# A unit's last attention step issued after one score group instead of two, and edge-pass loads cut in halves

## What is computed

```python
x = layernorm(x + attn(x, wq, wk_down, wv_down, wk_up, wv_up, wo))     # causal, T = 2048
nodes = {-1: x}
for c in range(6):
    nsrc = min(c + 1, 5); snode = c - nsrc
    q = ew[c,0] * (nodes[c-1]            @ We[eq] + be[eq])
    k = ew[c,1] * (nodes[snode]          @ We[ek] + be[ek])
    v = ew[c,2] * (nodes[snode + nsrc//2] @ We[ev] + be[ev])
    nodes[c] = act_w[c] * mha(q, k, v, Wq[c], Wk[c], Wv[c], Wo[c]) + q   # 8 heads of 128
x = layernorm(x + layernorm(nodes[5], ln_g, ln_b))
```

## Time and profile before

| what | value |
|---|---|
| median of 2 unprofiled runs | 8644.6 us (8638.22 to 8650.98) |
| the profiled execution's own time | 8620.5 us |
| its span on the slowest core (core 5) | 8619.4 us |
| spans of the eight cores | 8589.2 to 8619.4 us |
| mean granted TensorE clock, all cores | 0.809 to 0.813 of full speed |
| busy: PE, ACT, DVE, POOL | 70%, 28%, 20%, 1% |
| instructions | 67350 |
| DMA, mean over the span | 32 GB/s |

### The profile page before, as it was taken

How to read it: one execution, slowest core, us unless ns; L and a number is a source line. 1 busy time by engine, 2 the same in 40 slices (tenths; PEclk the granted TensorE clock), 3 DMA queues, 4 the chain that set the end, 5 groups by cost and what they waited for, 6 DMA issues and landing times.

```text
span 8619.4 us, 67350 instructions; the slowest of 8 cores (8589.2 to 8619.4 us)
## 1 busy us (share of the span) xinstructions
PE 6007.5 (70%) x22250; PEld 2193.1 (25%) x22250; DVE 1745.8 (20%) x2473; ACT 2453.4 (28%) x2040; POOL 59.1 (1%) x71
## 2 busy tenths in 40 slices
PE   6455577767776777877768967779777788646554
PEld 3111132222332222322223412224222233212111
DVE  3332122111121111131112131111301112231133
ACT  0222212433113332123441124331133421223322
POOL 0000000000000000000000000000000000000000
PEclk8677687888887888978889978889788889768777
DMA  3000031000320002310003200012200023000000
GB/s 74 25 25 25 10 83 25 10 10 10 74 49 5 20 10 43 90 25 10 10 10 74 69 15 10 10 44 69 49 15 10 10 44 91 13 25 0 25 25 20
DMA packets 148339, 271.72 MB, mean 32 GB/s; under 512 B 5216, under 2 KB 54688, under 8 KB 148022
## 3 DMA queue, kind: packets, MB, share of 16 engines
q0 software_dynamic: 69680, 111.42, 7.9%
q10 hardware_dynamic: 64928, 113.25, 4.1%
q1 hardware_dynamic: 13414, 42.76, 1.5%
HBM read 286.55 MB, written 67.11 MB: 41 GB/s over the span
## 4 chain that ended last, share of the span: by engine, by line
PE 58%; ACT 19%; DVE 10%; issue 7%; DMA 4%; DVEq 1%; ACTq 0%; SPq 0%; POOLq 0%
PE psS L57 27%; PE psA L57 22%; ACT Dm L57 15%; PE psY L57 5%; PE psM L57 4%; ACT rowb L57 3%; DVE LNw L57 3%; DVE Dm L57 2%; DVE rowb L57 2%; DVE psS L57 1%; DMA x1w<-x 1%; DMA A<-nsc 1%; DVE mask_sb L57 1%; DVE x1w L57 1%; DMA B<-x1b 1%
## 5 line engine op out<-in xcount | busy, mean ns | idle before, releaser
L57 ACT ACTIVATE Dm<-psS,negC 128x2048 bf16<-128x2048 f32 x848 | 1668.3, 1967 | 2844.5 <-PE psS L57 2645.6
L57 PE MATMUL psS<-A,B 128*128 128x512 bf16 x3392 | 1061.8, 443 | 707.0 <-ACT Dm L57 682.7
L57 PE MATMUL psY<-Dm,Cv 128*128 128x512 bf16 x1696 | 586.8, 482 | 360.2 <-DVE Dm L57 314.2
L57 DVE CAST mask_sb<-rowb 1x512 bf16<-1x512 f32 x192 | 79.7, 415 | 3718.1 <-ACT rowb L57 3718.1
L57 PE MATMUL psA<-Dm,Cv 128*128 128x512 bf16 x1696 | 570.8, 471 | 370.9 <-DVE Dm L57 328.0
L57 PE MATMUL psA<-Dm,Wb 128*128 128x512 bf16 (+1 forms) x2624 | 645.1, 403 | 83.6 <-DVE Dm L57 78.7
L57 PEld LDWEIGHTS psS<-A,B 128*128 128x128 bf16 x3392 | 337.0, 105 | 1411.2 <-issue 1299.5
L57 PE MATMUL psM<-Dm,on_b 128*1 128x512 bf16 x1808 | 573.0, 439 | 162.2 <-ACT Dm L57 154.4
L57 PE MATMUL psS<-Dm,Wb 128*128 128x512 bf16 (+1 forms) x2624 | 593.1, 379 | 0.0
L57 PE MATMUL psA<-Dm,on_b 128*1 128x512 bf16 (+1 forms) x1712 | 563.9, 461 | 8.0 <-DVE Dm L57 8.0
L57 PE MATMUL psA<-A,Wb 128*128 128x512 bf16 x1280 | 308.6, 397 | 157.2 <-DMA A<-nsc 92.0
(11 more groups left out here) (115 smaller groups left out, 3695.1 us busy)
## 6 DMA issues: line engine op xcount, KB each, us to landing
A<-nsc ACTq DMA_DIRECT2D x18, 2048.0 KB, 15.3
Wb<-ffn_We POOLq DMA_DIRECT2D x15, 2048.0 KB, 16.4
qsp<-Dm SPq DMA_DIRECT2D x6, 4096.0 KB, 26.3
Dm<-qsp ACTq DMA_DIRECT2D x24, 1024.0 KB, 6.6
nsc<-x1w POOLq DMA_DIRECT2D x20, 1024.0 KB, 11.3
x1w<-x ACTq DMA_DIRECT2D x32, 512.0 KB, 3.4
B<-x1b ACTq DMA_DIRECT2D x8, 2048.0 KB, 20.5
Wb<-ffn_Wv POOLq DMA_DIRECT2D x6, 2048.0 KB, 20.9
```

The source lines that it names most:

```text
L57: r = f(*a, **k)
```

## The change

Two independent edits. In `attn_unit` the tail of the unit before is now emitted between score group 0 and score group 1 for every unit with more than one group; before, units with three or four groups had it behind score group 1. This touches all 192 node units and the 16 units of layer 0 with three or four groups.

In the edge passes each [128, 8, 1024] load becomes two of [128, 8, 512], each with a semaphore of its own (dEa and the new dEb for A, dNk and the new dNkb for B). `proj_pass` gets an argument `ns_waits`: with it the loop runs over `ns` outside `m`, and each group of eight matmuls waits for the half that it reads.

```diff
-        def proj_pass(wslot, rhs_fn, evac_fn, tbs=range(NTB)):
+        def proj_pass(wslot, rhs_fn, evac_fn, tbs=range(NTB), ns_waits=None):
...
-            items = [(tb, m, ns) for tb in tbs for m in range(CH) for ns in range(2)]
+            if ns_waits is None:
+                items = [(tb, m, ns) for tb in tbs for m in range(CH) for ns in range(2)]
+            else:
+                items = [(tb, m, ns) for tb in tbs for ns in range(2) for m in range(CH)]
...
                 cv[0].wait(TE, cv[1])
+                if ns_waits is not None:
+                    ns_waits[ns][0].wait(TE, ns_waits[ns][1])
...
             emit_scores(0)
-            if ngrp == 2 and prev_tail is not None:
+            if ngrp > 1 and prev_tail is not None:
                 prev_tail()
             if ngrp > 1:
                 emit_scores(1)
-            if ngrp >= 3 and prev_tail is not None:
-                prev_tail()
             if prev_finish is not None:
                 prev_finish()
...
-                SE.dma_start(out=A3[:, :, (tb % 2) * 1024:(tb % 2) * 1024 + 1024],
-                             in_=fmv(src_dram)[:, :, tb * 1024:(tb + 1) * 1024]
+                SE.dma_start(out=A3[:, :, (tb % 2) * 1024:(tb % 2) * 1024 + 512],
+                             in_=fmv(src_dram)[:, :, tb * 1024:tb * 1024 + 512]
                              ).then_inc(dEa[tb % 2].h, 16)
                 dEa[tb % 2].n += 16
-                dEa[tb % 2].wait(TE)
+                SE.dma_start(out=A3[:, :, (tb % 2) * 1024 + 512:(tb % 2) * 1024 + 1024],
+                             in_=fmv(src_dram)[:, :, tb * 1024 + 512:(tb + 1) * 1024]
+                             ).then_inc(dEb[tb % 2].h, 16)
+                dEb[tb % 2].n += 16
```

More of the change, by code:

```diff
@@ L177, in build_nc @@
         dEa = [Sem(nc, ctx, "dEa0"), Sem(nc, ctx, "dEa1")]
+        dEb = [Sem(nc, ctx, "dEb0"), Sem(nc, ctx, "dEb1")]
+        dNkb = [Sem(nc, ctx, "dNkb0"), Sem(nc, ctx, "dNkb1")]
         dNk = [Sem(nc, ctx, "dNk0"), Sem(nc, ctx, "dNk1")]
@@ L202, in finish_all @@
                            (dA, GP), (dQr, GP), (dXf, GP), (dNk[0], GP), (dNk[1], GP),
+                           (dNkb[0], GP), (dNkb[1], GP), (dEb[0], GP), (dEb[1], GP),
                            (dX[0], GP), (dX[1], GP), (dEa[0], GP), (dEa[1], GP),
@@ L869, in edge_pass_full @@
                 gPE.wait(SE, pr)
-                SE.dma_start(out=A3[:, :, (tb % 2) * 1024:(tb % 2) * 1024 + 1024],
-                             in_=fmv(src_dram)[:, :, tb * 1024:(tb + 1) * 1024]
+                SE.dma_start(out=A3[:, :, (tb % 2) * 1024:(tb % 2) * 1024 + 512],
+                             in_=fmv(src_dram)[:, :, tb * 1024:tb * 1024 + 512]
                              ).then_inc(dEa[tb % 2].h, 16)
                 dEa[tb % 2].n += 16
-                dEa[tb % 2].wait(TE)
+                SE.dma_start(out=A3[:, :, (tb % 2) * 1024 + 512:(tb % 2) * 1024 + 1024],
+                             in_=fmv(src_dram)[:, :, tb * 1024 + 512:(tb + 1) * 1024]
+                             ).then_inc(dEb[tb % 2].h, 16)
+                dEb[tb % 2].n += 16
                 proj_pass(wslot,
                           lambda kc, tb_, ns: A3[:, kc, (tb % 2) * 1024 + ns * 512:(tb % 2) * 1024 + ns * 512 + 512],
-                          evac, tbs=[tb])
+                          evac, tbs=[tb],
+                          ns_waits=[(dEa[tb % 2], dEa[tb % 2].n),
+                                    (dEb[tb % 2], dEb[tb % 2].n)])
         for c, (eq, inq, ek, ink, ev, inv) in enumerate(NODES):
@@ L935, in build_nc @@
                     gPE.wait(SE, a_free[0])
-                    SE.dma_start(out=B3[:, :, (tb % 2) * 1024:(tb % 2) * 1024 + 1024],
-                                 in_=fmv(node_src[ink])[:, :, tb * 1024:(tb + 1) * 1024]
+                    SE.dma_start(out=B3[:, :, (tb % 2) * 1024:(tb % 2) * 1024 + 512],
+                                 in_=fmv(node_src[ink])[:, :, tb * 1024:tb * 1024 + 512]
                                  ).then_inc(dNk[tb % 2].h, 16)
                     dNk[tb % 2].n += 16
-                    dNk[tb % 2].wait(TE)
+                    SE.dma_start(out=B3[:, :, (tb % 2) * 1024 + 512:(tb % 2) * 1024 + 1024],
+                                 in_=fmv(node_src[ink])[:, :, tb * 1024 + 512:(tb + 1) * 1024]
+                                 ).then_inc(dNkb[tb % 2].h, 16)
+                    dNkb[tb % 2].n += 16
                     first_ev = [True]
@@ L954, in build_nc @@
                               lambda kc, tb_, ns: B3[:, kc, (tb_ % 2) * 1024 + ns * 512:(tb_ % 2) * 1024 + ns * 512 + 512],
-                              evac_ek, tbs=[tb])
+                              evac_ek, tbs=[tb],
+                              ns_waits=[(dNk[tb % 2], dNk[tb % 2].n),
+                                        (dNkb[tb % 2], dNkb[tb % 2].n)])
                 gEV.wait(TE)
```

## The result

The changed kernel takes 7755.2 us (median of 12 runs), the kernel before 8659.4 us (median of the 10 runs beside them). The ratio of the two times is 0.8929, 95% interval 0.8896 to 0.8963: 10.7% less time. The forecast was 7765 us, its range 7580 to 7970. Executions in which one die (cores 0 to 3 or 4 to 7) ran clearly longer at a lower clock are left out of the ratio and counted in the medians; the four quickest of the changed kernel's twelve lie at 7695.1 to 7696.7 us.

A forecast was written before the change was run, and what follows sets the result against it. PE was taken to bound the kernel, through its waits and its low clock. Savings of 754 + 60 + 65 = 879 us from 8620.5 gave 7741.5, plus 24.1 for unprofiled runs: 7765 us, range 7580 to 7970.

The forecast's parts named there:

- The two waits in the unit: Node attention unit: PE idles 2.27 us before score group 1 and 3.80 us before the first quad.
- the bare loads: Edge passes: eleven loads of A or B that PE awaits at once, 10.99 to 21.24 us each.
- One sign of the list: Profile after: PE's wait for ACT before score groups down from 683 to about 300 us.
- Schedule, 3.0 us per unit: Node unit at full clock: tail between score groups 0 and 1 shortens it from 18.8 to 15.75 us.
- Clock, 3.2 us down to 1.4: Node unit: low-clock loss falls to 1.4 us (bounds 0 and 3.2), one low stretch kept; unit 22.0 to 17.2 us.
- the first two: Rivals on the unit's clock: it stays up, 7556 us, chance 0.13; it loses as much as now, 8024 us, 0.17.
- part A's lower bound: Tail move in node attention: saving 754 us, bounds 552 to 956 from the clock term.
- rival 2: Node units: clock loses as much as now, 3.2 us per unit, 259 us less saved, 8024 us; chance 0.17.
- Per query block 31.4 us: Node attention: six units save 28.8 us, unit 1 saves 2.6, unit 0 nothing; 24 blocks give 754 us.
- Loads: Edge passes in halves: 63 us from nine loads, 9 from two, 7 off for late second halves: 65 us (0 to 90).
- The two beside a weight load: Loads behind a node's start, 21.0 and 21.2 us: gain only some 4.5 us each, 9 in all.
- The three terms: Savings: node attention 754 us, layer 0's two query blocks 60 (40 to 70), halved edge loads 65; 879 in all.

The follow-up runs named there:

- the filled kernel: Changed kernel plus ten extra matmuls, output never read, behind the finish in node units, in the idle before the first quad: 7500.2 us, ratio 0.8703.
- The filled kernels: Ten unread matmuls before the first quad, against the changed kernel: 7500.2 us; nine between score groups 0 and 1, against halved loads with old attention: 8398.2 us.
- the held-back weight load: Changed kernel with unit h-2's finish right behind score group 0 (7201.5 us), plus A passes' next weight load waiting for A's first half: 7174.6 us, ratio 0.8284.

## Why the prediction was right

*What bounds.* The two waits in the unit and the bare loads: right. Each was shortened or filled in a run of its own, and the time fell each time. One sign of the list was set wrong: PE's wait for ACT before score groups was to fall to about 300 us and fell to 380. It fell by 303, as the layout asks (1.82 us in 168 units is 306), but 683 less 303 is 380.

*Schedule, 3.0 us per unit.* Right: the full-clock pitch of the changed unit is 15.7 in the filled kernel, against the 15.75 worked out. Score group 1 still 3.29 us behind group 0, Ln held by exp of S0, 2.6 us of idle left before the first quad, exp of S1 late without cost: each as in the rows above.

*Clock, 3.2 us down to 1.4.* Right in the mean, and the least certain step. The filled kernels part the 3.2 into about 1.4 behind the first wait and the rest behind the second; what is left after the change is 1.5. But a low stretch behind each wait is the mean and not the rule of each unit. In the kernel before the pitches alternate between 22.9 and 21.2, and the wait of 2.27 us that has the clock at 0.53 behind it comes one unit later without it, the score group behind it taking 1.02 us:

```profile
5104.54 1.02 PE L57 MATMUL psS<-A,B 128*128 128x512 bf16 x4 [2.26 <-ACT Dm L57]
```

After the change the typical pitch is 17.1 to 17.3, with units of 15.7 and 18.2 among them. Why a wait brings the clock down in one unit and not in the next is open. No rival came true: a pitch of 15.8, or of 19 and more, would have shown the first two. In the bounds there is a slip: 144 units by 1.8 us are 259 us, so part A's lower bound is 495 us and not 552; rival 2 has it right.

*Per query block 31.4 us.* Measured 32.8, 787 us in all for 754. Layer 0: 76 us for 60. I had taken 30 us a block from the node units; 39.6 and 36.9 came. The granted clock over these two blocks rose from 0.71 to 0.85 and 0.82, over a node's block from 0.82 to 0.91: the masked loop had more low clock to lose.

*Loads.* Sized too cautiously: 83 us for 65. The first halves take 5.8 to 6.8 us in the chain, not 7.6 in the mean, so the nine give 76 in place of 63. The two beside a weight load give 7 in place of 9. The 7 us I took off for late second halves did not come on this core. The queues of the first pass of node 2 in the changed kernel, 3152 to 3162 us:

```profile
q0 software_dynamic: 603, 1.23, 81.3%
q10 hardware_dynamic: 600, 0.61, 22.8%
```

Turn for turn again, with half the bytes on ACT's side. So the second half comes late, but not by the 18 us worked out: in this pass the halves, issued 0.4 us apart, landed after 6.2 and 20.1 us, 14 apart, and in the nine short loads it is 13 to 16. PE's 17 us on the first half cover that; core 0 has no wait in its passes, and cores 1 and 5 have one each, of 0.2 us. The Trainium skill's rule of whole packets in turn (DMA: Bandwidth & Descriptors, section Queues, rings and completion order) fits both the 603 to 600 here and the held-back weight load, which gave the two long loads their 10 us back.

*The sum.* The three terms are 946 us where I had 879. The forecast was within 10 us of the median all the same, because the clock loss told above, which I had not put in, took some 60 us of it back; the four quickest runs stand 68 us under the forecast. The closeness of the hit is luck; its three terms were each within 28% of what was measured.

## What to carry to other kernels

Lay the loop out on paper for each engine's queue and look for two things: work that is ready and stands behind a wait, and a short instruction that stands in a queue behind a long dependence it does not share. The first was worth 4.8 of 22.0 us per unit here (3.0 of it schedule, the rest clock), the second 3.5 of the 17.2 left (2.0 schedule, 1.5 clock), by moving calls and adding one wait. Count the clock with the idle: a PE wait of 2 to 4 us in this loop cost some 1 to 2 us beyond itself in the mean of the units, and filling it with useless matmuls paid. And an engine's small instructions must fit the gaps one at a time: a pair of 0.7 us each delayed what a single one did not.

## Not expected

The third of four loads issued on ACT's queue took 2.2 us to issue and the fourth 13.6, where two took 1.00 us together before (timeline, ACT's queue, first pass of A in node 2, two windows):

```profile
3144.72 3.33 ACTq L57 DMA_DIRECT2D A<-nsc  x3
```

```profile
3148.08 13.59 ACTq L57 DMA_DIRECT2D A<-nsc  x1
```

ACT is held until 3161.7 us. It costs nothing here, because DVE evacuates these passes and ACT's next work is 51 us away, but on an engine with work behind the issues it would. I had priced the extra issues at half a microsecond each, and that was wrong. What limits the queue was not tried.

The granted clock of 0.79 and 0.81 through dense passes is neither of the two levels of the attention loop. The Trainium skill (TensorE: Matmul & The Clock Gate, Part 1) tells of a peak-current limit that takes a whole die to 13/16 of the clock, 0.81, when three or more cores run dense matmuls. The trace has that figure on the four cores of one die, but on cores 0 and 1 in the last node and on cores 2 and 3 only in layer 0; each core's times count from its own start, so whether these are the same moments cannot be read. The other die did the same dense passes at the full clock, and so did all eight cores in the profile of the kernel with the tail alone: all cores at work are not enough to bring it about here. What decides it, no run shows.
